# Distance term folded into the slopes, and weights summed from two blocks of six samples with 14 knots

## The reference

```
positions = clip(base + anchor + tanh(off) * 6, 0, q - 1)     # 16 heads, 12 samples a token
sk, sv = _sample(kh, positions), _sample(vh, positions)        # linear between two keys
scores = einsum(qh, sk) / sqrt(16)
scores = scores - rel_scale * |positions - arange(q)|
attn   = softmax(scores, axis=-1)                              # over the 12 samples
out    = einsum(attn, sv) @ wo.T + bo
```

## Time and profile before

| | |
|---|---|
| time, median of 3 runs | 1649.2 us (1646.07 to 1651.41) |
| span of the profiled execution | 1494.3 us, 35,841 instructions |
| the median time less that span | 154.9 us |
| TensorE busy | 1361.6 us, 91% |
| VectorE busy | 1280.2 us, 86% |
| ScalarE busy | 823.8 us, 55% |
| POOL busy | 804.3 us, 54% |
| DMA | 293.52 MB, mean 196 GB/s |

### The profile page before, as it was taken

How to read it: one execution, slowest core, us unless ns; L and a number is a source line. 1 busy time by engine, 2 the same in 40 slices (tenths; PEclk the granted TensorE clock), 3 DMA queues, 4 the chain that set the end, 5 groups by cost and what they waited for, 6 DMA issues and landing times.

```text
span 1494.3 us, 35841 instructions
## 1 busy us (share of the span) xinstructions
PE 1361.6 (91%) x13687; PEld 1085.4 (73%) x13688; DVE 1280.2 (86%) x1504; ACT 823.8 (55%) x1889; POOL 804.3 (54%) x566
## 2 busy tenths in 40 slices
PE   5998899984799999999999998999999978797988
PEld 4864565653688888888888886887888856675766
DVE  7837655556699999999999999999999999999961
ACT  2547687864445555555555554554555436574655
POOL 1001477773587766767666877768686651311111
PEclk9999999985999999999999999999999988898999
DMA  7933366564957676768677666767777679999897
GB/s 231 352 130 101 115 203 208 166 222 158 287 122 224 170 232 161 222 161 235 183 204 214 168 179 160 214 159 201 196 190 221 133 178 232 250 218 246 217 246 148
DMA packets 203481, 293.52 MB, mean 196 GB/s; under 512 B 24833, under 2 KB 160261, under 8 KB 203123
## 3 DMA queue, kind: packets, MB, share of 16 engines
q0 software_dynamic: 65792, 146.59, 38.5%
q1 hardware_dynamic: 134915, 144.84, 33.6%
q10 hardware_dynamic: 2672, 0.83, 0.2%
HBM read 182.83 MB, written 117.74 MB: 201 GB/s over the span
## 4 chain that ended last, share of the span: by engine, by line
DVE 48%; DMA 8%; PE 8%; issue 6%; SPq 5%; POOL 0%; ACT 0%; POOLq 0%; DVEq 0%
DVE gslope L1647 11%; DVE parts L1643 11%; DVE parts L1603 8%; DMA band<-band_rows 7%; DVE expert_mem L1569 5%; PE pB L1480 3%; DVE parts L1615 3%; SPq L1121 2%; DVE parts L1619 2%; DVE parts L1622 1%; PE pA L1465 1%; PE pY L1490 1%; DVE gslope L1700 1%; SPq L1115 1%; DVE wgt L1708 1%
## 5 line engine op out<-in xcount | busy, mean ns | idle before, releaser
L1175 POOL DMA_INDIRECT moe_rows<-expert_mem,token_of x142 | 324.9, 2288 | 76.2 <-issue 47.9
L1446 PE MATMUL pA<-xsT,expert_mem 128*128 128x256 f32 x1136 | 264.5, 387 | 22.6 <-DMA expert_mem<-in_w_l 15.5
L1156 POOL DMA_INDIRECT expert_mem<-xn_rows,token_of x142 | 222.3, 1566 | 96.8 <-issue 74.2
L1452 PE MATMUL pY<-expert_mem 128*128 x1136 | 265.7, 387 | 0.0
L1446 PEld LDWEIGHTS pA<-xsT,expert_mem 128*128 128x128 f32 x1136 | 220.3, 195 | 55.9 <-issue 20.0
L1446 PE MATMUL pB<-xsT,expert_mem 128*128 128x256 f32 x1136 | 256.8, 379 | 0.0
L1452 PEld LDWEIGHTS pY<-expert_mem 128*128 128x128 f32 x1136 | 211.1, 191 | 42.3 <-issue 16.2
L1446 PEld LDWEIGHTS pB<-xsT,expert_mem 128*128 128x128 f32 x1136 | 215.8, 190 | 29.3
L1643 DVE SCALAR_TENSOR_TENSOR parts<-pos_pair,prob 128x768 f32<-128x768 f32 x256 | 228.0, 953 | 1.1
L1647 DVE TENSOR_REDUCE gslope<-parts 128x256 f32<-128x3072 f32 x64 | 214.7, 3354 | 2.2
L1297 ACT ACTIVATE expert_mem<-pA,b1sel 128x256 f32<-128x256 f32 x284 | 111.3, 474 | 135.3 <-issue 93.2
(11 more groups left out here) (197 smaller groups left out, 2036.3 us busy)
## 6 DMA issues: line engine op xcount, KB each, us to landing
expert_mem<-in_w_l POOLq DMA_DIRECT2D x71, 1024.0 KB, 7.0
band<-band_rows SPq DMA_DIRECT2D x256, 96.0 KB, 5.5
S_rows<-stage SPq DMA_DIRECT2D x64, 376.0 KB
band_rows<-wgt SPq DMA_DIRECT2D x12, 1536.0 KB, 7.1
pos_pair<-pos_rows SPq DMA_DIRECT2D x28, 384.0 KB, 7.7
xn_rows<-stage SPq DMA_DIRECT2D x16, 512.0 KB, 5.4
v_rows<-stage SPq DMA_DIRECT2D x16, 512.0 KB, 4.2
moe_rows<-zeros POOLq DMA_DIRECT2D x4, 2048.0 KB
```

The costliest lines, as they stand in the source:

```text
L1156: nc.gpsimd.indirect_dma_start(out=xs[:, u, s], out_offset=None, in_=dram["xn"], in_offset=bass.IndirectOffsetOnAxis(ap=keep["inv"][:, 2 * ...
L1175: nc.gpsimd.indirect_dma_start(out=dram["moe"], out_offset=bass.IndirectOffsetOnAxis(ap=keep["inv"][:, 2 * n + s:2 * n + s + 1], axis=0), ...
L1446: mm = nc.tensor.matmul(dst[:, c], w1[:, 1 - u, k, o * HID + c * P:o * HID + (c + 1) * P], xsT[:, k], start=(k == 0), stop=(k == KC - 1))
L1452: mm = nc.tensor.matmul(pY[:, s], hid[:, h, c, s * P:(s + 1) * P], w2[:, c, ds(e * D, D)], start=False, stop=(s == 1 and c == HC - 1))
```

## The change

The distance term. -rel_scale * |p| is itself piecewise linear with a bend at 0. It is now added to the slopes: ScalarE adds `rel_fall` (-2 rel_scale * 4) in place to the slopes of the knots from 0 up, and `rel_low` (rel_scale * 4) to the copies `base`, `last4` and `tail4`. The 14th part, its Abs and its scaling go; the score tree has 13 parts (6 + 6, 3 + 3, 2 + 2, 1 + 1). `bends` now waits for that addition (`leaned`); the reloads of the slopes wait for `posT_ready` in place of `dist_set`.

The weights. The twelve samples are taken in two blocks of six; `front_block` stores the positions of the second block 2 lower (so L788 becomes two instructions of 96 elements in place of one of 192). Fourteen products replace sixteen. The sum over samples is no longer a TENSOR_REDUCE for every four knots but three additions over all fourteen at once, within each block of six: 3 + 3, then element 0 + element 1, then + element 2. `join_blocks` adds the two blocks, shifted by two knots; for the outer knots a block's share of the probability (`mass`) stands in. One difference now writes all of `gslope`.

```diff
-                for a in range(GROUP):
-                    ins = V.tensor_scalar(pos[:, u, a], pos[:, u, a], base_of(n, a), None, ALU.subtract)
+                    by_half = pos[:, u, a].rearrange("p (h b r) -> p b h r", b=WBLOCKS, r=WB)
+                    V.tensor_scalar(by_half[:, 0], by_half[:, 0], base_of(n, a), None, ALU.subtract)
+                    ins = V.tensor_scalar(by_half[:, 1], by_half[:, 1], base_of(n, a), float(WBLOCKS), ALU.subtract, ALU.subtract)
...
-                sp.wait_ge(dist_set, it)
+                sp.wait_ge(posT_ready, it)
...
-                for dst, first in ((base, 0), (last4, KNOTS - BLOCKS)):
-                    nc.scalar.activation(dst[:].rearrange("p b (g h) -> p g b h", h=HPAIRS), slope[:, :, first:first + BLOCKS],
-                                         ACT.Identity)
+                nc.scalar.activation(slope[:, :, REACH:], slope[:, :, REACH:], ACT.Identity, bias=rel_fall[:, 0:1]).then_inc(leaned, 1)
+                nc.scalar.activation(base[:].rearrange("p b (g h) -> p g b h", h=HPAIRS), slope[:, :, 0:BLOCKS], ACT.Identity,
+                                     bias=rel_low[:, 0:1])
+                act.wait_ge(leaned, it + 1)
+                nc.scalar.activation(last4[:].rearrange("p b (g h) -> p g b h", h=HPAIRS), slope[:, :, KNOTS - BLOCKS:], ACT.Identity,
+                                     bias=rel_low[:, 0:1])
...
-                dist = parts[:, PARTS - 1]
-                nc.scalar.activation(by_block(dist), by_token(posn), ACT.Abs).then_inc(dist_set, 1)
-                act.wait_ge(dist_set, it + 1)
-                nc.scalar.activation(dist, dist, ACT.Identity, scale=rel_neg[:, 0:1]).then_inc(dist_ready, 1)
...
-                    dve.wait_ge(s_loaded, 16 * 2 * SUBS * it + 16 * 2 * SUBS)
...
+                dve.wait_ge(leaned, it + 1)
...
-                chain.count(V.tensor_tensor(parts[:, 0:7], parts[:, 0:7], parts[:, 7:14], ALU.add))
+                chain.count(V.tensor_tensor(parts[:, 0:6], parts[:, 0:6], parts[:, 6:12], ALU.add))
...
-                for i in range(BATCHED):
-                    j = batch * BATCHED + i
-                    ins = V.scalar_tensor_tensor(terms[:, i], at, float(j - REACH), prob[:], ALU.max, ALU.mult)
-                chain(ins)
...
-                chain(V.tensor_reduce(G[:, :, batch * BATCHED:(batch + 1) * BATCHED].rearrange("p t j -> p j t"),
-                                      terms.rearrange("p j (t r) -> p j t r", r=SAMPLES), AX.X, ALU.add))
+            def join_blocks(chain):
+                share = mass[:, :, 0]
+                V.tensor_tensor(G[:, WBLOCKS:W_KNOTS], sums[:, WBLOCKS:, :, 0], sums[:, 0:W_KNOTS - WBLOCKS, :, 1], ALU.add)
+                V.tensor_tensor(G[:, 0:WBLOCKS], sums[:, 0:WBLOCKS, :, 0],
+                                sums[:, 0, :, 1].unsqueeze(1).broadcast_to([P, WBLOCKS, TH]), ALU.add)
+                for j in range(W_KNOTS, KNOTS):
+                    V.scalar_tensor_tensor(G[:, j], share, float(j - REACH), sums[:, j - WBLOCKS, :, 1], ALU.mult, ALU.add)
+                chain(V.tensor_scalar(G[:, KNOTS], share, float(WBLOCKS), float(REACH - WBLOCKS), ALU.mult, ALU.add))
...
+                chain(V.tensor_reduce(mass[:].rearrange("p t b -> p (t b)"), prob[:].rearrange("p (q r) -> p q r", r=WB), AX.X, ALU.add))
+                chain(V.tensor_tensor(smax[:], mass[:, :, 0], mass[:, :, 1], ALU.add))
+                chain(V.reciprocal(smax[:], smax[:]))
+                V.tensor_tensor(mass[:, :, 0], mass[:, :, 0], smax[:], ALU.mult)
+                chain(V.tensor_tensor(pairs(prob[:]), pairs(prob[:]), each_sample(smax[:]), ALU.mult))
+                weigh(it, range(0, 5))
+                also("weights 0")
+                weigh(it, range(5, 10))
+                also("weights 1")
+                chain(weigh(it, range(10, W_KNOTS)))
+                chain(V.tensor_tensor(terms[:, :, 0:3], terms[:, :, 0:3], terms[:, :, 3:6], ALU.add))
+                also("weights 2")
+                chain(V.tensor_tensor(terms[:, :, 0], terms[:, :, 0], terms[:, :, 1], ALU.add))
+                chain(V.tensor_tensor(terms[:, :, 0], terms[:, :, 0], terms[:, :, 2], ALU.add))
+                join_blocks(chain)
+                also("weights 3")
...
-                chain(V.tensor_tensor(gslope[:, :, 1:KNOTS], G[:, :, 1:KNOTS], G[:, :, 0:KNOTS - 1], ALU.subtract))
-                chain(V.tensor_scalar(gslope[:, :, KNOTS], gslope[:, :, KNOTS], -1.0, float(REACH), ALU.mult, ALU.add))
+                chain(V.tensor_tensor(gslope[:, :, 1:KNOTS + 1].rearrange("p t j -> p j t"), G[:, 1:], G[:, 0:KNOTS], ALU.subtract))
```

63 lines of the change are left out of this document (30 added, 33 removed).

## The result

The changed kernel takes 1659.1 us (median of 7 runs, 1654.18 to 1663.04) beside 1648.5 us of the kernel before on the same chip (median of 7, 1642.01 to 1651.41). The ratio is 1.006, with a 95% interval of 1.0041 to 1.0078: slower, by 0.6%. The forecast was 1641.8, with a range of 1631 to 1656.

The account below looks back on a forecast made before the run. The prediction took TensorE to bound the expert stage and DMA the tail. Its terms, +0.5 - 1.2 - 4.7 - 2 = -7.4 us, took 1649.2 to 1641.8 us, with a range of 1631 to 1656.

Parts of the forecast that it names:

- VectorE's step: VectorE per 512-token group: 4.5 us saved, 67.4 to 62.9 us, taking single-element accesses at 1.04 ns each.
- rival B: VectorE: single-element strides are slow, 1647 to 1651 us or up to 1696; sign, 1,792-element additions above 2.9 us; chance 0.1.
- The second doubt: First tree addition, three of every six elements: might suffer from its addresses too, 0 to 4.1 us more a step.
- The expert stage is TensorE's.: Expert stage: TensorE sets the pace, 65.0 us a step; VectorE's saved time gives nothing there by itself.
- (a): Start of the expert stage: shorter `prepare(1)` without Abs and scaling lets pair 3 start 1.2 us earlier.
- (b): End of the expert stage: TensorE's wait for the last gate (3.2) and slow matmuls after it (1.5) go, 4.7 us.
- (c): SP's queue: step 11's weights and slopes issue earlier, taking 2 us (none to 4) off the tail's DMA work.
- They give nothing more.: Tail: VectorE's four steps, 4.5 us shorter each, then wait for ScalarE's units and exponents, so no further gain.
- Front: Before the expert stage: splitting 64 subtractions of 192 elements into 128 of 96 costs 0.5 us.
- A: SP's DMA bursts at step ends fall badly, delaying TensorE's expert weights; 1644 to 1667 us, likeliest 1650; chance 0.2.
- C: Nothing gained: the tail's DMA landing order sets the end and gives the gains back; 1646 to 1649 us; chance 0.1.
- D: Every saved VectorE microsecond counts: 1577 us, held excluded; small form at most 12 us more gain, 1629; chance 0.05.

Follow-up runs that it names:

- contig: Changed kernel with later tree additions, joining and last difference on neighbouring addresses, same element counts, sums not the reference's; 0.9848 of the kernel before.
- reduce6: Changed kernel with each block of six samples summed by one reduction of 5,376 elements instead of the addition tree; 0.9941 of the kernel before.
- expert_skip: Kernel before with only two of four weight batches in steps 0 to 11, 14 us less VectorE work a step; 0.9869 of the kernel before.
- dist_only: Kernel before with only the distance term moved into the slopes, four reductions kept; 0.9939 of the kernel before.
- best: Changed kernel with one reduction per block of six and the base subtraction kept as one instruction of 192 elements; 0.9938 of the kernel before.
- reduce_pad: Changed kernel with one reduction per block of six, plus three idle 768-element reductions in each of steps 0 to 11; 0.9987 of the kernel before.
- tail_skip: Kernel before with two of four weight batches left out in steps 12 to 15 only; 1.0002 of the kernel before.
- after_again: Changed kernel, untouched, run again beside the kernel before where that takes about 1497 us; ratio 1.0082, 1509.2 us.
- units: Changed kernel with the third unit of step 13 done one place later, after the first tree addition; 1.0052 of the kernel before.
- exp_later: Changed kernel with the exponentials of steps 14 and 15 after tail tiles 29 and 45 instead of 28 and 42; 1.0033 of the kernel before.
- before_again: Kernel before, unchanged, traced again on the chips of the follow-up runs; one run, 1494.9 us.
- twin: Kernel before with its 3,072-element reductions replaced by two-input additions of 3,072, leaving out the sums over samples; 0.9986 of the kernel before.
- pos_only: Kernel before with only the base subtraction split into two instructions of 96 elements; 0.9992 of the kernel before.
- sample_major: Changed kernel's arithmetic with positions, exponentials and products laid out sample by sample, in runs of 16 or 32; 0.9865 of the kernel before.

## Why the prediction was wrong

**VectorE's step: the step that failed.** "The unknown is the address pattern ... I take 1.04: L1701 is within 10 ns of it and is the nearer operation." It is 1.85 ns an element, the scan's figure of the earlier trace rows and the forecast's own upper bound; the two additions take 3.47 us each, where "above 2.9" was to mean rival B. The terms: two additions of 1,792 at 3.47 for 2.01 (+2.9), the difference (+0.8), the joining (+0.6), the small ones of `join_blocks` (+0.2): 4.5 us a step, all of the 4.5 that were to be saved. L1701 misled, as a row of 64 elements is mostly the fixed cost of an instruction, and the 150 ns taken off it are those of other operations. Contig shows the same operation with neighbouring results:

```profile
L1655 DVE TENSOR_SCALAR bend<-mass x16: 181/185/188, 469.5 to 1416.1; 128x64 f32<-128x64 f32 x16
```

With scattered results its median is 216 ns in reduce6 (L1656) and 226 in the earlier trace rows. Against 185 the latter is 41 ns more over 64 elements, 0.64 ns each; with 1.04 it makes 1.7 (an estimate). So L1701 spoke for the scan's figure, not against it.

The second doubt, the first tree addition, was groundless: 5.84 us for runs of three, 5.76 for contiguous ones.

The Trainium skill, "SBUF — State Buffer", section "Specifications (TRN2)", says that an access that crosses to a new 16-byte line pays. For single elements the runs agree: 24 bytes or more apart they cost 1.85 ns, in reads (L1710) and in writes (L1717). Runs of three in every six cost 1.06 and runs of 16 nothing extra. The forecast named the rule and set it aside on one row.

**"The expert stage is TensorE's."** Half right. A floor at TensorE's pace exists, with VectorE standing at the gates (34.2 us in contig, 148.0 in expert_skip). But the kernel before stands some 10 us above it (842.7 against 833), and the forecast gave 1.2 (a) and 4.7 (b) for that. dist_only shows the slope: 0.8 us a step, 11.6 in the stage and 9 in the time. The list of waits misled: TensorE in the earlier trace rows waits for no gate, since the lag comes due only at the end, all at once and on a slowed clock. With the step at 67.2 the changed kernel gets nothing of it, and (b)'s waits stay, 7.5 and 2.0 us in its two profiles. In contig, reduce6, best and expert_skip, where VectorE is ahead, no gate wait is left, as (b) said. (a) is seen too: TensorE's waits for xsT are 2.9 to 5.8 us in the six profiles that have the Abs, and none to 2.5 in the twelve without; what that is worth in time isn't told apart.

**(c) SP's queue.** The mechanism is seen in expert_skip (the same store, 12 us ahead) and there worth 7.5 us by the profile and 10 by the time, where 2 were counted "(none to 4)". reduce_pad against reduce6 shows no such gain, so its size stays between nothing and ten. The changed kernel, with VectorE as late as before, gets nothing of it.

**"They give nothing more."** For saved time this holds in the kernel before (tail_skip, 1.0002). The forecast looked only at VectorE waiting for ScalarE there, not at ScalarE waiting for VectorE. That is where most of the slower comes from, as far as the runs show: `exponent` waits for wgt, the evacuations stand behind it in the same queue, and 5 to 7 us of the tail are lost (tails of 288.9, 289.2 and 289.0 in after, after_again and units; 283.2 and 282.1 with the exponentials later). In time the move takes the ratio from 1.006 and 1.0082 to 1.0033 and 1.0047, between 0.1 and 0.5%.

**Front.** +0.5 was counted; the time shows nothing, to some 2 us, and the profiles 1.6.

**The rivals.** B happened at its place and at the lower of its prices (4.3 us, measured 4.5), though its 1647 to 1651 missed the tail's loss. A did not show in the profile after (9.8 us of waits in its window against 9.7), but after_again has 14.9 there and exp_later 21.4, where before_again has 5.9; part of the open rest may be A in small pieces. C and D did not come; but had the addresses cost 1.04, the gain would have been contig's 23 us, nearer to D's 20 than to the forecast's 7.4. The time would have been some 1623 us (an estimate, 0.9848 of 1648.5), below the range. So the forecast had a second fault, what a saved microsecond of VectorE is worth, which would have shown without the first.

**Open.** exp_later is still 0.33% slower than the kernel before, about 5 us. It is not the step's length (reduce_pad), and not GpSimd's slowing alone (twin); for the front pos_only leaves 0.13%. In the mean of the five profiles with the change's tree the expert stage is 845.5 us, in that of five with the step of before (before, before_again, pos_only, tail_skip, twin) 843.1; a difference of 2.4 is within the scatter. The waits for expert weights are the place where it would be looked for next: the five profiles of kernels with the change's tree have 7 to 16 of them, all others 3 to 5, the first left out in each. What makes them more is not shown.

## What to carry to other kernels

Before a layout is chosen for a tree of additions, price it by the length of its contiguous runs: single 4-byte elements cost VectorE 1.85 ns, runs of three in every six 1.06, runs of 16 or more 1.05, and a change of layout (sample_major) turned a loss of 0.8% into a gain of 1.35%. Don't take such a price from a row of 64 elements, and take the fixed cost off a row only if it is that of the same operation; where two rows disagree by 1.5 times, as here, keep both as separate forecasts. A list of waits that ends before the stage's end doesn't show a lag that comes due there. When the work inside a step is put in another order, look also for the engine whose in-order queue holds a wait for its end, and for whatever stands behind that.

## What the runs showed of the hardware

- VectorE's instructions can slow GpSimd: with reductions replaced by additions of two inputs in SBUF at equal length (twin), a gather takes 1.81 us in place of 1.49 to 1.57 and a weight load's issue 1.21 in place of 0.98. The additions also write twelve times as many results. The Trainium skill, "GPSIMD Engine Reference", section "Specifications", says that GpSimd shares its way to SBUF with such instructions of VectorE; the run agrees, though it can't tell the second input from the writing.
- A reduction whose outputs are scattered (896 for 5,376 inputs) takes 5.75 us, as the contiguous addition of 5,376 does (5.77): scattered results, one for six inputs, cost nothing that shows.
- The front is some 150 us longer in some conditions, for the kernel before as well. In the profile after, TensorE idles 105.6 us before the small matmuls pS, put down to issue; in before_again 3.3. What makes it so is not shown.
- In the profile after, sixteen matmuls take 3.72 us after a wait of 2.05 us, and 6.57 after one of 5.42; the granted clock is 0.66 from 1355 to 1365 us. In before they take 5.23 after 3.17 us.
